# A pad of 128 bytes in front of XT, and bg placed in front of m, in an attention and mixture-of-experts layer

## The reference

```python
x = x + _layernorm(_L0_attn_ref(_layernorm(x), w_qkv, w_proj, b_proj))
x = x + _layernorm(_L0_ffn_ref(_layernorm(x), gate_w, Wg, Wu, Wd, Sg, Su, Sd))
...
# attention: one head of 256
scores = einsum('bqh,bkh->bqk', q, k) * 0.25
out = einsum('bqk,bkh->bqh', softmax(scores), v)
out = swapaxes(out, 1, 2).reshape(Bn, Sn, H)
out = einsum('bsh,eh->bse', out, w_proj) + b_proj
...
# experts: each of the 16 takes its 1024 best rows of the 8192
g = einsum('ecd,eid->eci', xg, Wg)
u = einsum('ecd,eid->eci', xg, Wu)
h = gelu(g) * u
eo = einsum('eci,edi->ecd', h, Wd) * topk_weight
...
# shared expert on all rows
shared = gelu(h_s @ Sg.T) * (h_s @ Su.T) @ Sd.T
```

## Time and profile before

| what | value |
|---|---|
| three runs, median | 1977.57 us (1977.18 to 1979.3) |
| profiled execution, first to last instruction | 1975.7 us |
| mean granted TensorE clock | 0.996 |
| TensorE matmuls (PE), busy | 1948.8 us, 99% of the span |
| TensorE weight loads (PEld), busy | 1657.2 us, 84% |
| VectorE (DVE), busy | 1366.5 us, 69% |
| ScalarE (ACT), busy | 1036.0 us, 52% |
| GpSimd (POOL), busy | 523.8 us, 27% |

### The profile page before, as it was taken

One profiled execution on the slowest core, in us unless ns is written; L12 is line 12 of the kernel. 1 busy time (PEld: TensorE's weight loads), 2 busy tenths in 40 slices (PEclk: granted clock), 3 DMA queues, 4 the chain that ended last, 5 costly groups with the idle time before them and its releaser, 6 DMA issues.

```text
span 1975.7 us, 29127 instructions
## 1 busy us (share of the span) xinstructions
PE 1948.8 (99%) x10638; PEld 1657.2 (84%) x10638; DVE 1366.5 (69%) x2602; ACT 1036.0 (52%) x1929; POOL 523.8 (27%) x626
## 2 busy tenths in 40 slices
PE   7999999999999999999999999999999999999997
PEld 6888888888888888888888888888888888888886
DVE  6777787777776778667676766656565656565647
ACT  4457576666655434445444544545454545445455
POOL 0031132123120001222432333243234323332246
PEclk9999999999999999999999999999999999999999
DMA  3103323333243111434434443443435344434566
GB/s 129 54 33 108 76 98 108 97 100 114 66 162 130 65 65 47 130 79 103 87 87 102 93 98 77 108 87 96 96 89 106 86 105 92 101 83 99 157 214 171
DMA packets 153338, 197.38 MB, mean 100 GB/s; under 512 B 104448, under 2 KB 121088, under 8 KB 145152
## 3 DMA queue, kind: packets, MB, share of 16 engines
q1 hardware_dynamic: 127824, 158.00, 25.6%
q0 software_dynamic: 25392, 37.77, 12.1%
HBM read 114.38 MB, written 59.34 MB: 88 GB/s over the span
## 4 chain that ended last, share of the span: by engine, by line
PE 67%; DVE 2%; POOL 1%; issue 1%; ACT 0%; DVEq 0%; ACTq 0%; POOLq 0%
PE mo_psD L1626 12%; PE mo_psG L60 7%; PE mo_psU L60 7%; PE mo_psU L62 7%; PE mo_psG L62 7%; PE mo_psG L61 7%; PE mo_psU L61 7%; PE mo_psD L1628 6%; PE mo_psD L60 1%; PE mo_psD L62 1%; PE mo_psD L61 1%; PE mo_psX L1351 1%; DVE mo_F L1940 1%; POOL mo_H_lo L2279 0%; POOL mo_rs L2289 0%
## 5 line engine op out<-in xcount | busy, mean ns | idle before, releaser
L1755 ACT ACTIVATE mo_HF<-mo_psG 128x512 f32<-128x512 f32 x320 | 191.3, 598 | 401.6 <-PE mo_psU L62 375.1
L2261 POOL DMA_INDIRECT ACC<-OUT,mo_GI x128 | 201.7, 1576 | 642.0 <-DVE OUT L2050 630.4
L1967 DVE TENSOR_TENSOR mo_HF<-mo_psU,mo_HF 128x512 f32<-128x512 f32 x320 | 220.4, 689 | 210.7 <-ACT mo_HF L1755 206.5
L1626 PE MATMUL mo_psD<-wd,mo_H_hi 128*128 128x512 f32 x1024 | 360.8, 393 | 0.2 <-DVE OUT L2050 0.2
L1628 PE MATMUL mo_psD<-wd,mo_H_lo 128*128 128x256 f32 x1024 | 289.3, 283 | 0.0
L60 PE MATMUL mo_psG<-mo_XT_hi,wg_hi 128*128 128x512 f32 x640 | 255.5, 399 | 0.4 <-DVE mo_HF L1967 0.4
L60 PE MATMUL mo_psU<-mo_XT_hi,wu_hi 128*128 128x512 f32 x640 | 253.5, 396 | 0.0
L62 PE MATMUL mo_psU<-mo_XT_hi,wu_lo 128*128 128x512 f32 x640 | 252.7, 395 | 0.0
L62 PE MATMUL mo_psG<-mo_XT_hi,wg_lo 128*128 128x512 f32 x640 | 252.6, 395 | 0.0
L61 PE MATMUL mo_psG<-mo_XT_lo,wg_hi 128*128 128x512 f32 x640 | 252.4, 394 | 0.0
L61 PE MATMUL mo_psU<-mo_XT_lo,wu_hi 128*128 128x512 f32 x640 | 252.4, 394 | 0.0
(11 more groups left out here) (354 smaller groups left out, 4154.6 us busy)
## 6 DMA issues: line engine op xcount, KB each, us to landing
X1a<-wg_in SPq DMA_DIRECT2D x16, 1024.0 KB, 5.2
X1a<-wu_in SPq DMA_DIRECT2D x16, 1024.0 KB, 4.8
X1a<-wd_in SPq DMA_DIRECT2D x16, 1024.0 KB, 4.8
XN<-XG SPq DMA_DIRECT2D x8, 1088.0 KB, 4.2
X<-x_in SPq DMA_DIRECT2D x8, 1024.0 KB, 5.4
out_dram<-X SPq DMA_DIRECT2D x8, 1024.0 KB, 6.4
XN2T<-xn2T SPq DMA_DIRECT2D x8, 1024.0 KB, 5.1
X1a<-xt_in SPq DMA_DIRECT2D x7, 1024.0 KB
```

The source lines that it names most:

```text
L1626: pe.matmul(psD[:, t % 2, :], h_hi, wd_both[:, it, :, :].rearrange("p z d -> p (z d)"), start=(it == 0), stop=False)
L1755: a.activation(HF[:, it % 2, :], psG[:, it % 2, :], ACT.Gelu).then_inc(s_gelu, 1)
L1967: v.tensor_tensor(HF[:, it % 2, :], psU[:, it % 2, :], HF[:, it % 2, :], ALU.mult).then_inc(s_mul, 1)
L2261: g.indirect_dma_start(out=io["ACC"], out_offset=bass.IndirectOffsetOnAxis(ap=GI[n % 2][:, 4 * tb + t:4 * tb + t + 1], axis=0), in_=OUT[:, ...
```

## The change

A tensor `lead` of 32 float32 numbers (128 bytes) a partition is made in moe in front of XT; nothing reads or writes it. In build, bg (64 bytes) is made in front of m instead of behind it. XT, HF, H, XG0 and everything behind them in moe so start 128 bytes higher, m starts 64 bytes higher, and attention's tensors behind bg stay where they were. The instructions, their order on each engine, their sizes and their waits are the same.

```diff
@@ moe @@
         wd = [wd_both[:, :, z, :] for z in (0, 1)]
+        new("lead", [P, 32])
         XT = [pair(f"XT{i}", [P, KD, 512]) for i in range(2)]
@@ build @@
-            c.wv, c.m = ([sa(f"{n}{z}", [P, KD, w], F32R) for z in (0, 1)] for n, w in (("wv_", ROW), ("m_", D)))
+            c.wv = [sa(f"wv_{z}", [P, KD, ROW], F32R) for z in (0, 1)]
             c.bg = sa("bg", [P, E])
+            c.m = [sa(f"m_{z}", [P, KD, D], F32R) for z in (0, 1)]
```

## The result

The changed kernel takes 1963.68 us (median of 5 runs, 1962.41 to 1964.0) against 1977.57: 13.9 us less, a ratio of 0.9926 with a 95% interval of 0.9915 to 0.9937. The forecast was 1956.2 us, in a range of 1947 to 1969. The span of the profiled execution fell from 1975.7 to 1962.0 us.

A forecast was written before the change was run, and what follows sets the result against it. TensorE, busy 1948.8 of 1975.7 us, was taken as the bound, so matmul start spacing sets the time. Terms 16.5 + 1.4 + 0.5 + 1.1 + 1.5 + 0.4 = 21.4 us took the median from 1977.57 to 1956.2 us, range 1947 to 1969.

The forecast's parts named there:

- The forecast's case: Whole kernel: gate/up, m and down products at operand distance 0 run faster, giving 1956.2 us; chance 0.72.
- It settles late: Rival: gate/up runs stay at the start-up level of 230.0 ns and down does not move; 1968.4 us, chance 0.12.
- The distance is not the cause: Rival: levels belong to the products, by surroundings or absolute places; nothing changes, 1977.6 us, chance 0.09.
- The new distance locks onto the upper level: Rival: gate/up and down rest at the slow level of V pairs at distance 0; 1996.9 us, chance 0.07.
- Experts' gate and up: Expert blocks, 3072 matmuls: 232.4 to 226.7 ns each, less nine start-up matmuls at 230.0 per block; gain 16.5 us.
- First shared blocks: Gate and up in the first twelve shared blocks, 576 matmuls at the start-up level; gain 1.4 us, bounds 0 and 3.3.
- Last blocks: Gate and up in the last four blocks, 192 matmuls, where TensorE already waits; gain 0.5 us, bounds 0 and 1.1.
- Experts' down: 1024 pairs landing at 345.7 ns (gain 5.0 us) or 353.3 (loss 2.8 us); middle taken, gain 1.1 us.
- Shared down: Down of the shared expert, 744 matmuls now 118.6 ns each, 2 ns less each; gain 1.5 us, bounds 0 and 3.
- Product by m: 192 matmuls going from 229.3 to 226.7 ns with a start-up each round; gain 0.4 us, bounds 0 and 0.5.
- Nothing new is late in the middle of the program: Other engines using the moved tiles: costed at nothing, since load rises only from 66% to 67% if TensorE gets 2% faster.
- the sum's "poor" corner: Poor bounds of the sum: 16.0 us experts, 0.7 shared blocks, less 2.8 in down; 13.9 us gain, 1963.7 us.

## Why the prediction was right, and where its terms were off

The forecast's case came out, and the three rivals didn't. The steady gate/up level is 226.7 ns, to the tenth what a product of the same shape showed at distance 0 in the kernel before. One reading of the three levels had a wrong sign (m at 64 is m at 192), which did no harm, because every product went to 0. "It settles late" fails, since a run is at 226.7 after some nine matmuls. "The distance is not the cause" fails by the shift of everything and by the seven sizes of the pad (none among them): one program, same instructions, 1963.7 to 1978.4 us by 64 bytes of placement. "The new distance locks onto the upper level" was wrong for gate/up, its main part, and right for the down, its small one.

Term by term, predicted against measured gain:

1. Experts' gate and up, 16.5 against 13.4 us. The level was right. The start-up was mis-sized: the first nine of an unbroken run average 233.2 ns, not 230.0, so 58 ns a block instead of 30, 0.9 us more over 32 blocks. The new wait for VectorE, with the restart behind it, is 0.23 us in each of the nine blocks that have it (22.06 us on average, against 21.82 in the nine others without a break), 2.1 us together. That is 3.0 of the 3.1 us. No experiment took that wait away; it stands in nine blocks of every kernel here whose gate/up is at 226.7 or 228.9 ns and in none of the slower ones.
2. First shared blocks, 1.4 against 2.4 us. The sum set a start-up level after the change (230.0) against a settled one before it (232.4). But the search's matmuls restart these runs in both kernels: all 576 average 236.8 ns before and 232.6 after, 4.2 ns less instead of 2.4. Inside the bounds 0 to 3.3.
3. Last blocks, 0.5 against 0.7.
4. Experts' down, +1.1 against -2.1 us. The upper bound of the loss was 2.8; all 32 blocks went to the upper level of the earlier trace rows, 353.3 ns. Taking the middle of two discrete levels is the step that failed.
5. Shared down, +1.5 against -0.9 us, outside the bounds of 0 and 3. The nearest row, the 256-column half of the V pairs, was no guide: by itself in `mm3` a 256-column stream at distance 0 takes 120.0 ns. A loss should not have been excluded.
6. Product by m, 0.4 against 0.2 us in the seven rounds at the full clock. The level fell as said (226.7), but it came from 228.9, and the start-up got longer.
7. "Nothing new is late in the middle of the program" failed. It was argued from VectorE's average, 319 us free in 930. In the steps in which VectorE also centres weights (1.2 us, L88) it is late by a fifth of a microsecond once TensorE is 2% faster, and TensorE waits.

The terms' misses, 3.1 - 1.0 - 0.2 + 3.2 + 2.4 + 0.2 = 7.7 us, are the 7.7 us between the forecast span (1954.3) and the measured one (1962.0). The mechanism was right, but the forecast gain of 21.4 us is one and a half times the measured one, and two of its terms had the wrong sign; the result equals the sum's "poor" corner of 13.9 us by chance, since its parts (16.0, 0.7 and -2.8) are not the measured ones.

The rule weighed in the prediction, of the Trainium skill's "TensorE: Matmul & The Clock Gate" ("Step-by-step: what each phase is for"), that loading the next tile's weights doesn't steal SBUF read bandwidth from the running matmul, had been taken to mean that the distance has no price. In that sense it doesn't hold here by the measurement: with the same instructions, the distance between load and stream moves a 512-column fp32r matmul between 226.7 and 233.3 ns. Whether read bandwidth is what is lost, no run shows. What happens inside SBUF to bring this about was not tried and stays open. So does why a run at one distance has two levels, and what picks one of them.

## What to carry to other kernels

Where TensorE has no idle time and each matmul loads its own weights, read start-to-start times, not busy time, and compare products of one shape at different operand places: the difference is a free experiment that the trace already holds. Set each load's distance to the stream that runs while it loads, product by product, since a good place for 512 columns is a bad one for 256; here that gave 1.5% where one common pad gave 0.7%. And cover for a faster bottleneck is to be looked up in the fullest step, not in a stretch's average.

## What the hardware showed that wasn't expected

- The effect of the distance repeats every 256 bytes and has a sign: 226.7 ns at 0, 233.3 at 32 and at 64, 232.4 at 128, 228.9 at 192, for fp32r streams of 512 columns with loads of 128.
- A settled run is periodic: at distance 0 the distances are 226, 227, 227 ns over and over, at 128 they run through 231, 231, 229, 230, 232, 241, 232 in a cycle of about seven.
- The same pair of instructions at the same distance has two stable levels, 346.7 and 353.3 ns at distance 0, and stays in one for a whole run of an expert's down. The lower one is the sum of the single levels there, 226.7 + 120.0.
- With high and low placed apart the pair's level is the sum of the two best single ones, 226.7 + 113.3 = 340.0 ns. With the two swapped it is 350.0, a little over the sum, 228.9 + 120.0 = 348.9.
- The first nine matmuls of a gate/up run cost more or less by the product in front: 233.2 ns each behind a down at distance 0, 228.7 behind one at 128.
